# Attention of a four-stage transformer block: six score banks in rotating couples and a new table of places

## The reference, cut to what matters

```
L0: x += g * selfattn(ln(x)) @ Wo       (rope, mask)
    x += g * crossattn(ln(x), ctx) @ Wo  (mask)
    x += g * (gelu(ln(x) @ W1) @ W2)
L1: x += crossattn(ln(x), ln(ctx)) @ Wp
L2: x += g * selfattn(ln(x)) @ Wo;  x += crossattn(ln(x), ctx) @ Wo;  x += g * mlp(ln(x))
L3: x += gate * (mixture of 3 experts of ln(x) and attention over ctx) @ Wout
attn: s = q @ k.T / sqrt(8); a = softmax(s); a @ v          (16 heads of 8 features)
```

## Time and profile before

| | us |
|---|---|
| median of 3 runs | 632.28 (631.93 to 633.33) |
| the profiled execution | 630.35 |
| its span, first to last instruction | 628.5 |
| PE busy | 553.0 (88%) |
| DVE busy | 441.5 (70%) |
| ACT busy | 408.6 (65%) |
| POOL busy | 219.7 (35%) |

### The profile page before, as it was taken

How to read it: one execution, slowest core, us unless ns; L and a number is a source line. 1 busy time by engine, 2 the same in 40 slices (tenths; PEclk the granted TensorE clock), 3 DMA queues, 4 the chain that set the end, 5 groups by cost and what they waited for, 6 DMA issues and landing times.

```text
span 628.5 us, 25631 instructions
## 1 busy us (share of the span) xinstructions
PE 553.0 (88%) x11207; PEld 312.6 (50%) x11207; DVE 441.5 (70%) x1156; ACT 408.6 (65%) x704; POOL 219.7 (35%) x324
## 2 busy tenths in 40 slices
PE   6888887999879987888788988899999989999997
PEld 2344344545435544455444654466455655575546
DVE  6879788748886778769876878688676786244223
ACT  3243636566767476865778476867998767657761
POOL 7333453524442254523543345352342341110000
PEclk9899999999999999999999999999999999999999
DMA  6902000000000000000000000000000000000000
GB/s 205 329 6 61 27 2 19 19 2 20 22 16 3 19 3 27 11 2 20 20 19 2 20 19 2 2 21 2 20 3 2 4 3 20 3 3 19 3 3 35
DMA packets 15350, 16.32 MB, mean 26 GB/s; under 512 B 1831, under 2 KB 13109, under 8 KB 14857
## 3 DMA queue, kind: packets, MB, share of 16 engines
q1 hardware_dynamic: 14664, 10.70, 5.5%
q10 hardware_dynamic: 576, 4.00, 1.7%
HBM read 13.60 MB, written 1.09 MB: 23 GB/s over the span
## 4 chain that ended last, share of the span: by engine, by line
PE 52%; ACT 22%; DVE 17%; issue 5%; SPq 1%; POOL 1%; DMA 1%; DVEq 0%; POOLq 0%; ACTq 0%
PE lin L1031 16%; ACT P L640 13%; PE big L1031 11%; PE big L1195 8%; PE avp L1220 7%; DVE mhl L870 4%; PE big L1174 3%; PE big L1202 2%; ACT xn L604 2%; ACT L640 2%; ACT L649 1%; ACT hid L649 1%; DVE onT L887 1%; DVE bst L813 1%; PE lin L1124 1%
## 5 line engine op out<-in xcount | busy, mean ns | idle before, releaser
L870 DVE TENSOR_REDUCE mhl<-big 128x8 bf16<-128x616 f32 (+1 forms) x160 | 149.5, 963 | 44.2 <-PE big L1174 42.3
L571 POOL TENSOR_TENSOR qm<-qT,hm 128x512 f32<-128x512 f32 x80 | 85.8, 1073 | 89.0 <-PE big L1202 41.6
L640 ACT ACTIVATE P<-big 128x1024 f32<-128x1024 f32 x64 | 62.0, 1021 | 62.5 <-PE big L1202 62.4
L1195 PE MATMUL big<-qm,kT 32*128 32x512 f32 x640 | 91.2, 640 | 0.0
L1220 PE MATMUL avp<-P,Vp 128*32 128x128 f32 x2560 | 87.3, 276 | 1.3 <-issue 1.3
L557 POOL TENSOR_TENSOR kbm<-kT,hm 128x308 bf16<-128x308 f32 (+1 forms) x80 | 69.9, 874 | 49.8 <-PE big L1174 27.1
L640 ACT ACTIVATE P<-big,padcol 128x1024 f32<-128x1024 f32 x64 | 67.8, 1110 | 26.4 <-PE big L1202 26.3
L534 POOL TENSOR_SCALAR rstd<-mv 128x4 f32<-128x4 f32 (+3 forms) x37 | 8.7, 236 | 213.9 <-DVE mv L819 213.7
L1220 PEld LDWEIGHTS avp<-P,Vp 128*32 128x32 f32 x2560 | 69.0, 110 | 22.3 <-issue 19.4
L1031 PE MATMUL lin<-hT,W 128*32 128x512 f32 (+2 forms) x608 | 78.0, 589 | 0.2 <-ACT hT L619 0.2
L1174 PE MATMUL big<-kbm,qb 32*128 32x308 bf16 (+1 forms) x320 | 51.0, 332 | 24.1 <-ACT P L640 24.0
(11 more groups left out here) (206 smaller groups left out, 876.9 us busy)
## 6 DMA issues: line engine op xcount, KB each, us to landing
gring<-gate_rows SPq DMA_DIRECT2D x20, 256.0 KB, 3.4
W<-in_w ACTq DMA_DIRECT2D x2, 1152.0 KB, 13.6
hid<-in_ws SPq DMA_DIRECT2D x2, 768.0 KB, 5.8
W<-in_w ACTq DMA_DIRECT2D x1, 1088.0 KB, 8.7
x<-in_x SPq DMA_DIRECT2D x4, 256.0 KB, 7.0
out<-x SPq DMA_DIRECT2D x4, 256.0 KB, 2.4
ctx<-in_ctx SPq DMA_DIRECT2D x4, 154.0 KB
ctxT<-in_ctxT SPq DMA_DIRECT2D x4, 154.0 KB
```

The lines of the kernel that those rows point to most:

```text
L571: nc.gpsimd.tensor_tensor(qm[:, j % 2], q.broadcast_to([128, 4, T]), mask.broadcast_to([128, 4, T]), ALU.mult).then_inc(qm_ready, 1)
L640: nc.scalar.activation(P[:, 8 * half:8 * half + 8, :], big[:, 2 * half:2 * half + 2, :].rearrange("p g (h q) -> p (g h) q", h=4), ACT.Exp, ...
L870: v.tensor_reduce(mhl[:].rearrange("p (g c) -> p g c", c=32)[:, 2 * half:2 * half + 2, 0:4], big[:, 2 * half:2 * half + 2, 0:4 * kw].rearr ...
L1195: mm(big[:, g, :].rearrange("p (h q) -> p h q", h=4), kT[s][r, b * kw:b * kw + 128], qm[r, j % 2], start=(a > 0), stop=False, skip_group_c ...
```

## The change

`big` grows to six banks, three couples; `avp` and `mtp` go. Couples rotate with the job number j: maxima scores of half 0 are in couple j, those of half 1 in couple j + 1, the transposed scores of heads 0 to 7 in couple j + 2, those of heads 8 to 15 in couple j again (all modulo 3). The turned maxima lie in a corner of couple j + 1, the values of P by V in a corner of couple j. `scores(j + 1, 0)` waits for no exps, `scores(j + 1, 1)` for `exps(j, 0)`, `av(j)` for `exps(j, 1)`, and `scores_t(j)` waits until `normalise(j - 1)` has read the values. `normalise(u)` moves on DVE from slot 4u + 4, behind turned(u + 1), to slot 4u + 3, before turned(u + 1). Two memsets that gave first permissions go. After the last job eight banks serve the linear stages instead of six. The whole table SLOTS is new; of it only some rows are shown.

```
+NATT = 6
 SLOTS = {
-    (0, 1): [0, 1, 4, 8, 11, 14],
-    (0, 2): [4, 9, 13, 22, 34, 47],
-    (1, 0): [6, 7, 12],
-    (2, 0): [10, 16, 16, 17, 19, 20, 22, 24, 27],
-    (2, 1): [32, 32, 36, 42, 44, 44, 44, 49, 51],
+    (0, 1): [0, 0, 5, 7, 8, 11],
+    (0, 2): [12, 13, 18, 23, 37, 47],
+    (1, 0): [8, 10, 15],
+    (2, 0): [9, 16, 19, 19, 20, 21, 23, 23, 27],
+    (2, 1): [30, 32, 32, 34, 36, 38, 39, 43, 51],
...
-        big = ps("big", [128, 4, 512])
-        avp = ps("avp", [128, 512])
-        mtpf = ps("mtp", [128, 512])
+        big = ps("big", [128, NATT, 512])
...
+        def pair_of(j, part):
+            return 2 * ((j + ("maxima 0", "maxima 1", "exps 0").index(part)) % 3)
+        def maxima_banks(j, half):
+            n = pair_of(j, f"maxima {half}")
+            return big[:, n:n + 2, :]
+        def exps_banks(j, half):
+            n = pair_of(j, "maxima 0" if half else "exps 0")
+            return big[:, n:n + 2, :]
+        def av_ap(j):
+            return big[:, pair_of(j, "maxima 0"), 0:2 * T]
+        def turn_ap(j):
+            return big[:, pair_of(j, "maxima 1"), 0:T]
...
-            v.memset(mT[:], 0.0).then_inc(av_free, 1)
-            v.memset(mhl[0:1, 0:1], 0.0).then_inc(st_free, 2)
...
-                dve.wait_ge(av_free, n + 1)
+                dve.wait_ge(av_free, n)
...
                     if s == 0:
                         if u > 0:
                             turned(u)
-                            normalise(u - 1)
-                    elif s < 3 and u + 1 < JOBS:
+                    elif s == 3:
+                        normalise(u)
+                    elif u + 1 < JOBS:
                         maxima(u + 1, s - 1)
-                elif kind == "END":
-                    normalise(JOBS - 1)
...
-                pe.wait_ge(st_free, job_turn(j, half, 2))
+                if half == 1 and j > 0:
+                    pe.wait_ge(st_free, job_turn(j - 1, 0, 2))
...
                 pe.wait_ge(m_ready, job_turn(j, 1, 2))
+                if j > 0:
+                    pe.wait_ge(av_free, job_turn(j - 1))
+                banks = [exps_banks(j, g // 2)[:, g % 2, :] for g in range(4)]
...
-                pe.wait_ge(st_free, job_turn(j, 1, 2) + 2)
-                pe.wait_ge(av_free, job_turn(j))
+                pe.wait_ge(st_free, job_turn(j, 1, 2))
```

More of the change, by code:

```diff
@@ L207, in result_of @@
     return "y" if u[0][0] == "m" and u[1][0] == "y" else u[1].rstrip("a")
-LIN_AT, _uses, _held, _ended, _next = {}, [0] * (NLIN + 4), set(), False, 0
+LIN_AT, _uses, _held, _ended, _next = {}, [0] * (NLIN + NATT), set(), False, 0
 for _kind, _u, _s in UNITS:
@@ L402, in build @@
         rows_done, rows_in = sem("rows_done"), sem("rows_in")
-        lin_full = [sem(f"lin_full{i}") for i in range(NLIN + 4)]
-        lin_free = [sem(f"lin_free{i}") for i in range(NLIN + 4)]
+        lin_full = [sem(f"lin_full{i}") for i in range(NLIN + NATT)]
+        lin_free = [sem(f"lin_free{i}") for i in range(NLIN + NATT)]
         ln_bn, ln_stats, ln_eps, ln_pow, ln_rstd, ln_xn = ([sem(f"{n}{s}") for s in range(NS)] for n in (
@@ L640, in exps @@
                 nc.scalar.activation(P[:, 8 * half:8 * half + 8, :],
-                                     big[:, 2 * half:2 * half + 2, :].rearrange("p g (h q) -> p (g h) q", h=4),
+                                     exps_banks(j, half).rearrange("p g (h q) -> p (g h) q", h=4),
                                      ACT.Exp, scale=SCALE, **hidden).then_inc(st_free, 1)
@@ L870, in maxima @@
                 v.tensor_reduce(mhl[:].rearrange("p (g c) -> p g c", c=32)[:, 2 * half:2 * half + 2, 0:4],
-                                big[:, 2 * half:2 * half + 2, 0:4 * kw].rearrange("p g (h k) -> p g h k", h=4), AX,
+                                maxima_banks(j, half)[:, :, 0:4 * kw].rearrange("p g (h k) -> p g h k", h=4), AX,
                                 ALU.max).then_inc(m_ready, 1)
@@ L875, in turned @@
                 dve.wait_ge(mt_full, job_turn(j))
-                v.tensor_copy(mT[:], mtpf[:, 0:T]).then_inc(mt_ready, 1)
+                v.tensor_copy(mT[:], turn_ap(j)).then_inc(mt_ready, 1)
             def normalise(j):
@@ L882, in normalise @@
                 dve.wait_ge(av_full, n)
-                v.transpose(avT[:], avp[:, 0:2 * T].rearrange("p (n q c) -> p q n c", n=2, c=32)).then_inc(av_free, 1)
-                dve.wait_ge(av_free, n + 1)
+                v.transpose(avT[:], av_ap(j).rearrange("p (n q c) -> p q n c", n=2, c=32)).then_inc(av_free, 1)
+                dve.wait_ge(av_free, n)
                 v.reciprocal(rden[:], avT[:].rearrange("p k (h d) -> p k h d", d=8)[:, :, 2:4, 0]).then_inc(rden_ready, 1)
@@ L1049, in keep_warm @@
                 for _ in range(n):
-                    mm(mtpf[:], oneb[:, 0:128], oneb[:], start=True, stop=True)
+                    mm(big[:, 5], oneb[:, 0:128], oneb[:], start=True, stop=True)
             pe.wait_ge(oneb_set, 1)
@@ L1159, in scores @@
                     pe.wait_ge(kbm_ready, job_turn(j))
-                pe.wait_ge(st_free, job_turn(j, half, 2))
+                if half == 1 and j > 0:
+                    pe.wait_ge(st_free, job_turn(j - 1, 0, 2))
+                banks = maxima_banks(j, half)
                 for g in (2 * half, 2 * half + 1):
-                    o = big[:, g, 0:4 * kw].rearrange("p (h k) -> p h k", h=4)
+                    o = banks[:, g % 2, 0:4 * kw].rearrange("p (h k) -> p h k", h=4)
                     if a == 0:
@@ L1179, in turn @@
                 pe.wait_ge(m_ready, job_turn(j, 1, 2))
-                strips(mtpf[:, 0:T], mhl[:], identb[:], start=True, stop=True, skip_group_check=True).then_inc(mt_full, 1)
+                strips(turn_ap(j), mhl[:], identb[:], start=True, stop=True, skip_group_check=True).then_inc(mt_full, 1)
             def scores_t(j):
@@ L1187, in scores_t @@
                 pe.wait_ge(m_ready, job_turn(j, 1, 2))
+                if j > 0:
+                    pe.wait_ge(av_free, job_turn(j - 1))
+                banks = [exps_banks(j, g // 2)[:, g % 2, :] for g in range(4)]
                 if a == 0:
                     for g in range(4):
-                        strips(big[:, g, :].rearrange("p (h q) -> p h q", h=4), identb[:],
+                        strips(banks[g].rearrange("p (h q) -> p h q", h=4), identb[:],
                                mkq[:].unsqueeze(1).broadcast_to([128, 4, T]), start=True, stop=False, skip_group_check=True)
@@ L1194, in scores_t @@
                     r = slice(32 * g, 32 * g + 32)
-                    mm(big[:, g, :].rearrange("p (h q) -> p h q", h=4), kT[s][r, b * kw:b * kw + 128],
+                    mm(banks[g].rearrange("p (h q) -> p h q", h=4), kT[s][r, b * kw:b * kw + 128],
                        qm[r, j % 2], start=(a > 0), stop=False, skip_group_check=True)
@@ L1201, in scores_t @@
                         r = slice(32 * g, 32 * g + 32)
-                        i = mm(big[:, g, hh * T:(hh + 1) * T], indb[r, hh, :], mT[r], start=False, stop=(hh == 3),
+                        i = mm(banks[g][:, hh * T:(hh + 1) * T], indb[r, hh, :], mT[r], start=False, stop=(hh == 3),
                                skip_group_check=True)
@@ L1210, in av @@
                 lin_taken(pe, f"p{a}", s, "v")
-                pe.wait_ge(st_free, job_turn(j, 1, 2) + 2)
-                pe.wait_ge(av_free, job_turn(j))
+                pe.wait_ge(st_free, job_turn(j, 1, 2))
+                o = av_ap(j)
                 if j == 0:
@@ L1219, in av @@
                         for g in range(4):
-                            i = mm(avp[32 * g:32 * g + 32, nb * T:(nb + 1) * T], Vp[s][:, b, 4 * g + hh, :],
+                            i = mm(o[32 * g:32 * g + 32, nb * T:(nb + 1) * T], Vp[s][:, b, 4 * g + hh, :],
                                    P[:, 4 * g + hh, :], start=(hh == 2 * nb), stop=(hh == 2 * nb + 1), skip_group_check=True)
```

## The result

The changed kernel took 641.12 us in the median of four runs (636.61 to 642.90), against 632.8 before. The ratio is 1.0122, with a 95% interval of 1.0063 to 1.0181. The prediction had 629.3, and a range up to 639. It is slower by some 1.3%, outside the range and not the way that was forecast.

A forecast was written before the change was run, and what follows sets the result against it. PE was taken as nearest to full (553.0 of 628.5 us), in a relay with ACT and DVE. Some 16 us of exp waits go, 19 come back for values and mT; all terms sum to -3.0, forecasting 629.3 us, range 618 to 639.

The forecast's parts named there:

- Every duration stays: Whole kernel: same matmuls, exps and reductions with the same shapes, so only waits differ; no change in durations counted.
- the clock is no cause: Jobs 8 to 79: granted clock 1.00, so it does not explain PE's 50.5 us idle there.
- signs of being wrong: Wrong if mT waits exceed 25 us, exp waits stay over 30, or xn, hT and hid waits become a large group.
- Waits for exps: PE's scores and P by V waiting for exps: counted 41.0 to 24.0, scaled by 38.6/41.0 to -16.0 us.
- Transposed scores for the values: PE waits until DVE transposes the values out of the shared couple: at most 0.48 us each, 30 passages, +10.7 us.
- Subtraction: PE's subtraction waits for mT because normalisation precedes its copy on DVE: 13.2 us in 44 passages, +8.7 us.
- Turn: PE's turn of the maxima waits for DVE: counted 8.2 to 7.3 us, -0.9 us.
- Output projection: PE's wait for the last job's values, ready a place earlier: -2.7 us at most, all of it taken.
- Jobs 0 to 7: First eight jobs: waits counted 21.2 to 16.5 us, half of the difference taken, -2.3 us.
- Tail: Behind the last job: removed memsets and two further banks gain 0.5 us, between 0 and 3.
- Rival 2: DVE's queue stands until P by V ends, delaying its units for POOL and ACT: about 637 us, chance 0.31.
- Rival 1: DVE gains more, normalising while it waits for P by V anyway: -12.3 us, 620 us, chance 0.19.

The follow-up runs named there:

- 48 fillers: Changed kernel plus unused 512-column matmuls on PE where its profile showed waits over 0.4 us for the turn or mT; 635.28 us, ratio 1.0046.
- delays alone: Kernel before plus four unused 128x512 products on DVE ahead of the second reduction of jobs 10, 22, 33, 43 and 57; 649.32 us.
- those delays filled: Kernel before with the same DVE delays, plus 10, 14, 12 and 10 unused matmuls before the turns of jobs 10, 22, 43 and 57; 642.54 us.
- the run with two fillers: Changed kernel plus two unused 512-column matmuls behind the turn wherever no PE unit lies between P by V and the turn; 643.54 us, ratio 1.0176.
- 61 fillers: Changed kernel with the 48 unused matmuls and 13 more, four before turns and nine behind them; 635.26 us, ratio 1.0046.
- The runs with the old table: Changed kernel with the table of before, 688.16 us; and kernel before with only the normalisation moved early on DVE, 694.12 us.

## Why the prediction was wrong

The forecast for the profiled execution was 627.3 us and it took 642.90. Of these 15.6 us, 10.8 are PE's busy time and 4.8 its idle time.

**"Every duration stays", and "the clock is no cause".** This step failed, and with it the larger part of the sum. I read in the earlier trace rows that the granted clock was 1.00 in the main stretch and took it as given for the changed kernel; the sum has no term for it. It should have asked what the new waits do to the clock. 10.8 us of PE's busy time appeared with the same matmuls. With 48 fillers the time falls by 6.1 us (641.34 to 635.28). With delays alone, put into the kernel before, 11.4 us of busy time appear, and with those delays filled 6.8 us of time go again. The Trainium skill's page "TensorE: Matmul & The Clock Gate", section "A second HAM failure mode: psum-queue depth-cycling", describes a kernel that cycles through PSUM banks, idles for a moment between groups of matmuls and has its clock fall and recover again and again. The profiles agree in the fall behind short waits close together (0.70, 0.89 and 0.97 us ahead of 183.0 in the profile after). The waits of half a microsecond behind the turns, which the run with two fillers took out, were not what brought it on here. I had not weighed that page.

None of the signs of being wrong that the prediction lists came: the subtraction waits 8.8 us (the limit was 25), the waits for exps are 21.7 (30), and those for ACT's xn, hT and hid grew only from 3.0 to 5.6. They all look at waits, and the loss lay elsewhere. The stretch from the first turn to the last P by V grew from 518.3 to 530.2 us, where I had it shrink by 2 to 3.

**The waits, term by term.** The count was sound where it was made with the right neighbours.
- Waits for exps: forecast -16.0, measured 38.6 to 21.7, -16.9. Right.
- Transposed scores for the values: forecast +10.7 in 30 passages, measured 11.2 in 28. Right. The bound of 0.48 us from the last job was about the right price, as long as DVE stands ready.
- Subtraction: forecast +8.7, measured 5.6 to 8.8, +3.2. Too high, and more so in jobs 8 to 79, which the forecast was for: 4.1 to 4.7 there.
- Turn: forecast -0.9, measured +3.3. Mis-sized by 4 us, and by 5 in jobs 8 to 79 (4.1 to 8.1). Job 10 alone has 3.18 of it.
- Output projection: forecast -2.7, measured 2.7 to 0.7. Right.
- Jobs 0 to 7: forecast -2.3, measured -1.0 of idle time. Tail: forecast -0.5, measured +0.2 of idle time. No run shows this term, and it had no source: the text ahead says that eight banks serve the linear stages behind the last job, but `_n = NLIN + 4 if _ended else NLIN` stands in both kernels, so it is six in both.

In sum the forecast was -3.0 us of idle time and the profile has +1.8. The waits named here make -1.2 of it over the whole span (-16.9 + 11.2 + 3.2 + 3.3 - 2.0), other listed waits some +1, and the rest lies in gaps too short for the list. In the run with 48 fillers it is +3.7 (633.9 - 565.7 + 11 - 75.5, the fillers taken as idle). So even nearly at the full clock the prediction's sign would have been wrong by a little: those runs are 2.5 us above the kernel before, and those with 61 fillers 2.9. Two steps failed, then: the clock, set at nothing, and the balance of the waits, where the turn was the term most under its measure.

**Rival 2** had the right side and the wrong mechanism. It put the loss into DVE's queue reaching POOL and ACT late, at 637. In the changed kernel PE's waits for such work stayed small (xn, hT and hid 5.6 us, before 3.0). The runs with the old table show what that queue does where units stand in front of the normalisation (42.4 us and 48.4 us of waits in place of 11.2 and 8.8). The new table mostly avoids it, at the price of other places: the rope unit of job 10 stands between two reductions and makes the longest wait of all. That too is DVE coming late, so a part of the 2.5 us that remain is of rival 2's kind. **Rival 1** was wrong: the turn's waits grew. The wait for the values in their corner cost 11.2 us, close to the 10.7 computed. By the Trainium skill's page "PSUM — Partial Sum Buffer", section "PSUM bank collisions raise a hardware error", two engines must keep out of one bank and quadrant whatever the columns; no run tried the corners without the wait, so none bears on that rule.

What stays open: why the same wait is followed by a low clock in one execution and not in another, and with it why the first four runs of the changed kernel scatter over 6 us (636.6 to 642.9). Only one execution of each series is profiled, two of the changed kernel in all. No run took out the waits that remain at the full clock, so the last 2.5 to 2.9 us are put down to them by count alone.

## What to carry to other kernels

When a change moves waits about on PE, look at PE's busy time before the idle time, and at the clock beside it: if the same matmuls are busy longer and the clock is lower, the loss is the clock, up to half a us for each us at 0.50. The longest single waits are the first suspects, then shorter ones that stand close together; the sum of all waits says little. A filler matmul of 0.2 us, put into a long wait and into a bank that is about to be overwritten, is a cheap test of that, and a partial cure. And a table of places fitted to one set of banks says nothing about another: exchange both or neither, and check first which engine's units stand in front of the instruction that frees a bank.

## What the runs showed of the hardware

Long single waits of PE often come with a clock of 0.50. In the kernel before with delays that was so at three of the four (3.47, 2.99 and 2.53 us): the stretch at 0.50 began about 1 us behind the end of the first wait and within the last half microsecond of the two others. The fourth fell into a stretch at 0.50 already. At the turn of job 57, which ran at 401.19 after waiting 2.53 us, the stretches read (window, length, busy of PE and the others, clock):

```profile
398.00:400.70 2.70, 0.66 (x26) 0.39 (x16) 2.70 (x6) 0.55 (x1) 0.00 (x0) 1.00 0.00 0
400.75:407.50 6.75, 6.31 (x76) 3.70 (x80) 5.00 (x18) 3.16 (x5) 2.78 (x6) 0.50 0.00 0
```

With these waits filled the clock stayed at 1.00 there. It is no rule for each single wait: the one of 1.84 us near 24.5 is followed by a stretch at 0.50 in the profiles before and after, but not in the one with 48 fillers, and the one of 1.9 us for mT near 94.5 in the kernel before has none behind it, while it has one in both runs with delays. Shorter waits close together did it too: some 0.9 and 0.6 us ahead of 172.1 and 254.0 in the run with delays. Filling the waits of half a microsecond alone changed nothing of the mean clock (0.983 in place of 0.984).

Some instructions of DVE between SBUF tiles took longer while POOL was at work. In the window from 101.00 to 104.40 of the changed kernel POOL is busy for 2.95 of 3.40 us, and DVE's sum of 128x512 took 1.24 us and its cast 1.15, where the medians are 0.69 and 0.43. In the run with new banks and the old table the residual sum of the same shape took 1.58 us, with POOL at work from 180.13 on; its mean is 0.78. It depends on what POOL does. Beside POOL's products (`qm`, `kbm`) the residual sum took 1.05 to 1.39 us three times in the kernel before and 1.2 to 1.6 us four times in the run with new banks and the old table; beside POOL's power function for `rstd` it took 0.69, at 62.07 of the kernel before and at 93.23 of the changed one. None of this was tried by itself. By the medians it made the wait of job 10 longer by some 1.3 us, an estimate.
